# Normalised rows of a two-layer block made by ScalarE with a scale and a bias per row

## The reference

```python
def _layernorm(x, axis=-1, eps=1e-05):
    m = jnp.mean(x, axis=axis, keepdims=True)
    v = jnp.var(x, axis=axis, keepdims=True)
    return (x - m) / jnp.sqrt(v + eps)
...
    x = x + jnp.tanh(g_xattn[0]) * _L0_xattn_ref(16, 128, 256, L0_xattn_time_decay, L0_xattn_time_first, _layernorm(x, axis=-1), ctx_2048)
    x = x + jnp.tanh(g_ffn[0]) * _L0_ffn_ref(_layernorm(x, axis=-1), L0_ffn_W_q, ...)
    x = x + jnp.tanh(g_xattn[1]) * _L1_xattn_ref(_layernorm(x, axis=-1), ctx_2048, ...)
    x = x + jnp.tanh(g_ffn[1]) * _L1_ffn_ref(_layernorm(x, axis=-1), ...)
    return x
```

## Time and profile before

| | |
|---|---|
| median of 3 runs | 586.26 us (586.02 to 588.57) |
| the profiled execution | 589.14 us, of which the span 587.3 us |
| busy in the span | TensorE 477.8 us (81%), VectorE 402.3 us (68%), ScalarE 173.8 us (30%), GpSimd 144.1 us (25%) |
| TensorE's granted clock | 0.92 of full speed on average |

### The profile page before, as it was taken

One profiled execution on the slowest core, in us unless ns is written; L12 is line 12 of the kernel. 1 busy time (PEld: TensorE's weight loads), 2 busy tenths in 40 slices (PEclk: granted clock), 3 DMA queues, 4 the chain that ended last, 5 costly groups with the idle time before them and its releaser, 6 DMA issues.

```text
span 587.3 us, 7047 instructions
## 1 busy us (share of the span) xinstructions
PE 477.8 (81%) x2142; PEld 367.5 (63%) x2150; DVE 402.3 (68%) x1049; ACT 173.8 (30%) x363; POOL 144.1 (25%) x141
## 2 busy tenths in 40 slices
PE   1755989778999679899999979999868599999720
PEld 1432468656767567668776867777646487888510
DVE  6999777999868997867859683997825343223332
ACT  2601434121233111141222123213334147555210
POOL 4942113551104010000000010000275105004664
PEclk9857999989999889989999989999978699999775
DMA  8150012300000049000000000111121416555653
GB/s 296 69 186 0 2 30 93 94 1 0 2 0 1 1 135 304 1 1 0 2 1 0 2 0 28 54 55 54 64 90 71 127 36 195 165 168 171 180 182 123
DMA packets 34277, 43.79 MB, mean 75 GB/s; under 512 B 3009, under 2 KB 28098, under 8 KB 34242
## 3 DMA queue, kind: packets, MB, share of 16 engines
q1 hardware_dynamic: 31170, 34.96, 18.6%
q0 software_dynamic: 3072, 8.39, 4.7%
HBM read 24.99 MB, written 18.35 MB: 74 GB/s over the span
## 4 chain that ended last, share of the span: by engine, by line
PE 36%; issue 6%; POOL 5%; DVE 4%; DMA 3%; ACT 2%; POOLq 0%; SPq 0%; ACTq 0%; DVEq 0%
PE ring L600 6%; PE acc L564 5%; PE ring L751 3%; PE ring L820 2%; PE ring L767 2%; PE ring L619 2%; PE ring L540 2%; POOL x_rows L1456 2%; PE ring L541 2%; PE ring L542 2%; PE ring L800 2%; POOL q_f L1465 2%; PE ring L584 1%; DMA main_b<-x_rows 1%; PE ring L811 1%
## 5 line engine op out<-in xcount | busy, mean ns | idle before, releaser
L564 PE MATMUL acc<-w_down,act_s 128*128 128x256 f32 x384 | 91.0, 384 | 0.7 <-DVE act_s L1258 0.7
L564 PEld LDWEIGHTS acc<-w_down,act_s 128*128 128x128 f32 x384 | 73.9, 193 | 12.7 <-DVE act_s L1258 1.1
L540 PE MATMUL ring<-xt_h,up_l 128*128 128x512 f32 x160 | 72.3, 452 | 5.4 <-ACT logits L921 3.0
L1426 POOL TENSOR_TENSOR rstd<-var_eps,minus_half 128x4 f32<-128x4 f32 x16 | 16.6, 1035 | 215.5 <-DVE var_eps L1054 215.5
L541 PE MATMUL ring<-xt_l,up_h 128*128 128x512 f32 x160 | 65.0, 406 | 0.0
L542 PE MATMUL ring<-xt_h,up_h 128*128 128x512 f32 x160 | 64.9, 406 | 0.0
L971 ACT ACTIVATE act_s<-ring 128x512 f32<-128x512 f32 x48 | 28.7, 598 | 113.8 <-PE ring L542 113.8
L1241 DVE SCALAR_TENSOR_TENSOR act_s<-act_s,ring 128x512 f32<-128x512 f32 x48 | 32.7, 681 | 29.4 <-ACT act_s L971 22.6
L600 PE MATMUL ring<-up_e,act_s 128*128 x184 | 48.4, 409 | 4.7 <-issue 3.5
L1456 POOL DMA_INDIRECT x_rows<-main_a,slots x32 | 31.5, 985 | 64.5 <-ACT main_a L988 32.4
L600 PEld LDWEIGHTS ring<-up_e,act_s 128*128 128x128 f32 x184 | 35.7, 204 | 11.3 <-issue 6.9
(11 more groups left out here) (239 smaller groups left out, 948.6 us busy)
## 6 DMA issues: line engine op xcount, KB each, us to landing
main_b<-x_rows SPq DMA_DIRECT2D x22, 256.0 KB, 2.9
y_rows<-act_s SPq DMA_DIRECT2D x22, 256.0 KB, 2.2
x_rows<-k_r SPq DMA_DIRECT2D x1, 3968.0 KB, 14.5
x_nat<-in_x SPq DMA_DIRECT2D x8, 256.0 KB, 4.5
stage<-in_w_mlp SPq DMA_DIRECT2D x8, 256.0 KB, 2.7
up_e<-in_w_moe SPq DMA_DIRECT2D x8, 256.0 KB, 2.6
out_x<-x_nat SPq DMA_DIRECT2D x8, 256.0 KB, 2.3
x_rows<-k_r SPq DMA_DIRECT2D x1, 1920.0 KB, 19.7
```

Of the source, the lines that this page charges most:

```text
L540: pe.matmul(out, wl, xh, start=first, stop=False, skip_group_check=True)
L564: last = pe.matmul(acc[t // 2][:, t % 2, :], act_s[n % RING][:, tok], w_down[:, u, :], start=u == 0 and t % 2 == 0, stop=final, skip_group ...
```

## The change

ScalarE makes the rows of all norms but the very first (`wkv_in 0`) by 4 activations `Identity(scale * x + bias)` with scale = rstd and bias = -mean * rstd, where VectorE did. For the bias, VectorE writes `minus_mean` (one instruction more, while the two additions of eps become one), and GpSimd multiplies it by rstd after the power, having waited for its own power (`rstd_made`); only then is `rstd_ready` raised. rstd and the bias of `route_in` go straight to `rstd2` and `shift2`, so the copies of line 1069 are gone. In the list the steps keep their places.

```diff
+NORM_DVE = [("wkv_in", 0)]
...
+                if APPLY.get(kind) == part and step not in NORM_DVE:
+                    n = XN_ORDER[step]
+                    xn_free(act, n)
+                    act.wait_ge(rstd_ready, 1 + (LAST_STATS[g] if kind == "mlp_in" else STATS_ORDER[step]))
+                    seqs = main_seqs(g) if kind in ("mlp_in", "attn_in", "moe_in") else prep_seqs(g)
+                    for t, b in enumerate(seqs):
...
+                        last = act.activation(xn[n % 2][:, t, :], x_nat[:, b, :], ACT.Identity, bias=m, scale=r)
+                    last.then_inc(xn_ready, 1)
...
-                for p in range(2):
-                    b = seqs[2 * p]
-                    var = mean_rstd[:, b:b + 2, 1] if keep else mv[:, n, 2 * p:2 * p + 2, 1]
-                    last = dve.tensor_scalar(var_eps[:, n, 2 * p:2 * p + 2], var, LN_EPS, None, ALU.add)
-                last.then_inc(var_ready, 1)
...
+                dve.tensor_scalar(minus_mean[:, n, :].rearrange("p (q b) -> p q b", q=2), mean, -1.0, None, ALU.mult)
+                dve.tensor_scalar(var_eps[:, n, :].rearrange("p (q b) -> p q b", q=2), var, LN_EPS, None,
+                                  ALU.add).then_inc(var_ready, 1)
...
-                if step[0] == "route_in":
-                    for p in range(2):
-                        b = seqs[2 * p]
-                        last = dve.tensor_copy(rstd2[:, b:b + 2], rstd[:, o % 2, 2 * p:2 * p + 2])
-                    link(last)
...
-                elif APPLY.get(kind) == part:
+                elif APPLY.get(kind) == part and step in NORM_DVE:
                     normalize(step, seqs)
...
-                    pool.tensor_tensor(rstd[:, n % 2, :], var_eps[:, n % 2, :], minus_half[:, :],
-                                       ALU.pow).then_inc(rstd_ready, 1)
+                    r, m = scales(step)
...
+                    pool.tensor_tensor(r, halves[0], halves[1], ALU.pow).then_inc(rstd_made, 1)
+                    pool.wait_ge(rstd_made, n + 1)
+                    pool.tensor_tensor(m, halves[2], r, ALU.mult).then_inc(rstd_ready, 1)
```

More of the change, by code:

```diff
@@ L217 @@
 STATS_ORDER = {s[:2]: n for n, s in enumerate(s for s in SCHED if s[0] in APPLY and s[0] != "mlp_in" and s[2] == 0)}
+LAST_STATS = {f: max(n for s, n in STATS_ORDER.items() if s[0] == "route_in" and s[1] // 2 == MAIN_FIRST[f] % 8 // 4)
+              for f in range(NG)}
 ALL_UNITS = [("mlp", f, u) for f in range(NG) for u in range(MLP_UNITS)]
@@ L304, in build @@
         rstd = sb("rstd", [P, 2, GT])
+        shift = sb("shift", [P, 2, GT])
+        minus_mean = sb("minus_mean", [P, 2, GT])
         v_t = [sb(f"v_t{c}", [P, GN]) for c in range(C)]
@@ L469, in weigh_values, with by_prep, scales, xn_free @@
             return eng.tensor_tensor(va[:, 0], va[:, 1], v[c][:, :].rearrange("p (t j) -> p t j", t=GT), ALU.mult)
+        def by_prep(table, g):
+            if len(table.shape) == 3:
+                return table[:, :, :].rearrange("p (q b) t -> p q b t", q=2)[:, :, 2 * g:2 * g + 2, :]
+            return table[:, :].rearrange("p (q b) -> p q b", q=2)[:, :, 2 * g:2 * g + 2]
+        def scales(step):
+            if step[0] == "route_in":
+                return by_prep(rstd2, step[1]), by_prep(shift2, step[1])
+            n = STATS_ORDER[step] % 2
+            return tuple(table[:, n, :].rearrange("p (q b) -> p q b", q=2) for table in (rstd, shift))
+        def xn_free(eng, n):
+            if n >= 2:
+                prev = [s for s, k in XN_ORDER.items() if k == n - 2][0]
+                full(eng, (prev, "T", C - 1))
         def free_sem(key):
@@ L883, in _ @@
                 ee_a, ee_b = ee_a_of[g], ee_b_of[g]
-                if kind == "wkv_in" and part == 2:
+                if APPLY.get(kind) == part and step not in NORM_DVE:
[4 more added lines that the diff above has]
+                    for t, b in enumerate(seqs):
+                        if kind == "mlp_in":
+                            r, m = rstd2[:, b:b + 1], shift2[:, b:b + 1]
+                        else:
+                            r, m = (table[:, t // 2, t % 2:t % 2 + 1] for table in scales(step))
+                        last = act.activation(xn[n % 2][:, t, :], x_nat[:, b, :], ACT.Identity, bias=m, scale=r)
+                    last.then_inc(xn_ready, 1)
+                elif kind == "wkv_in" and part == 2:
                     if g == 0:
@@ L1425, in _ @@
                     pool.wait_ge(var_ready, n + 1)
[L1426 to L1427 removed]
+                    r, m = scales(step)
+                    halves = [table.rearrange("p (q b) -> p q b", q=2)
+                              for table in (var_eps[:, n % 2, :], minus_half[:, :], minus_mean[:, n % 2, :])]
+                    pool.tensor_tensor(r, halves[0], halves[1], ALU.pow).then_inc(rstd_made, 1)
+                    pool.wait_ge(rstd_made, n + 1)
+                    pool.tensor_tensor(m, halves[2], r, ALU.mult).then_inc(rstd_ready, 1)
                 elif kind == "wkv_in" and part == 2:
```

21 lines of the change are left out of this document (10 added, 11 removed).

## The result

The changed kernel takes 584.62 us (median of 20 runs, 582.69 to 588.59), the kernel before beside it 587.43 us (20 runs, 584.84 to 589.35). The ratio is 0.996, 95% interval 0.994 to 0.998: 0.4% or 2.4 us faster, within the 0.5% that counted as no change. A second comparison on another occasion gave 0.999, interval 0.998 to 1.001 (587.89 us, 12 runs, against 588.64). The forecast was 2.3 us faster, 584.0.

What follows compares the result with a forecast made beforehand. VectorE was taken as the bound at 14.5 to 57 and 110 to 142 us, elsewhere mostly TensorE or transfers. Places summed to -1.3 us, with clock terms -2.3, from 586.26 to 584.0 us; range 579.5 to 589.0.

Steps and rivals of the forecast that it cites:

- The likeliest case: Whole kernel: gains in the MLPs outweigh losses at the start and before the first MLP, -2.3 us; chance 0.52.
- Start: ScalarE's rows of wkv_in 1 delay the exponentials; VectorE's line 467 starts 2.1 us later, an idle 0.69 absorbed: +1.4 us.
- Before the first MLP: ScalarE's 8 rows delay the key/value evictions and TensorE, +1.4 us; the longer wait makes the clock fall, +1.1.
- First MLP: Rows of wkv_in 2 and mlp_in 1 leave VectorE's queue, so TensorE's waits of 4.00 and 1.50 us shrink: -2.8 us.
- the term of wkv_in 2: First MLP: its rows leave VectorE, 1.84 us less the overlap and ScalarE's slightly longer rows: 1.5 us gained.
- Second MLP: Multiplication and longer rows of route_in 2 cost +0.6 us; at its end 8 ScalarE rows delay a tanh, +0.4.
- Third MLP: Rows of attn_in 0 no longer hold up routing on VectorE, -1.3 us; full clock behind the shorter wait, -1.7.
- Fourth MLP: Rows of attn_in 2 come earlier, -1.3 us; 0.4 counted for the clock here and in the first MLP together.
- The end, +0.3: At attn_in 3 the multiplication stands in the queue of GpSimd's sends: +0.3 us.
- A dear bias: Rival: GpSimd's multiplication costs 1.04 us instead of 0.3, paid eight times, +3.6 us, 589.9; loss from 0.6 us on; chance 0.14.
- The rival that the relief of the first MLP is lost: TensorE's waits there hang on something else just behind: 2.8 us less gain, +0.5 us, 586.8; chance 0.14.
- the first rival, in which the relief goes further: Clock stays full behind all shortened waits and does not fall at 76 us: -6.4 us, 579.9; chance 0.20.

Runs made afterwards that it cites:

- all, with bias: Changed kernel with all rows made by VectorE again, as before the change, while GpSimd still makes every bias; ratio to the kernel before 1.000 (0.998 to 1.002).
- the values later: Changed kernel with wkv_in 2 and mlp_in 1 rows on VectorE, GpSimd weighing wkv_in 2's values only after VectorE reduced the routing's pair products; ratio to before 1.003.

## Why the prediction was right in sum and wrong in its parts

The likeliest case came true in sign, in size and in most of its places, and in the sum that was partly luck. The forecast of -2.3 us lies between the two profiles of the changed kernel, -5.6 and -1.9 us of span. The first MLP and the fourth gave 2.5 and 1.0 us more than their terms; the start lost 0.8 us more, and the low clock at 79 us up to 2.3 us more, by the execution.

- **Start**, predicted +1.4. Line 476 (467 before) started at 16.73 us, 2.2 later, as forecast. All of that ran through: the power of route_in 0 came at 57.15 instead of 54.95 us, 40.4 us behind that instruction in both kernels. With the bias alone ("all, with bias") it came at 55.68, and with wkv_in 1 back on VectorE at 55.89, so some 0.7 us is the bias and 1.3 the rows of wkv_in 1; route_in 0, which I had given nothing, cost nothing that shows (route_in 1 at 70.34 with both back, 70.37 with wkv_in 1 alone). The step that failed is the idle 0.69 us of VectorE at 20.80, which I took off. The gap is gone, but k_e behind it took 1.42 instead of 0.66 us. Both ended 0.28 us behind GpSimd's `q_f`, 21.46 behind 21.18 and 23.65 behind 23.37, and GpSimd had been moved by the same 2.2 us. So the gap was no slack, and it looks like the collision found in the first MLP; no experiment tests it here.
- **Before the first MLP**, predicted +1.4 for the wait and +1.1 for the clock. From the power to k_e it was 4.81 us and is 6.34, 1.5 more: right. The fall of the clock came as forecast. Its price was mis-sized: I priced one low stretch of 3.4 us, as the rows of before at 250 us had it. Seven profiles gave 25.2 to 28.6 us for the stretch, 27.0 in the mean, so against the 25.2 of the one with full clock 1.8 us on average for the clock and up to 3.4.
- **First MLP**, predicted -2.8. The step that failed is the term of wkv_in 2: 1.5 us predicted, 4.0 measured; that of mlp_in 1 was 1.3 and is 1.3. I counted the rows that go, and took the instructions behind them as they stood. The rows are right: they bring the two instructions of the routing 1.6 us nearer to the power. But those two and the comparisons behind them were slowed by GpSimd, and moving them forward took them out from under it: 1.9 us for the two, and 0.4 for the next (2.27 to 1.86). The kernel with the values later shows 2.0 us with the rows left on VectorE. The forecast wait of 2.5 us for the routing's transposes is gone altogether, and one of 2.18 us stands behind it. A clue was in the rows: the same rows of xn took 1.84 us beside GpSimd and 1.38 alone, and I used it for the rows only. The Trainium skill (GPSIMD Engine Reference, Key points) says that GpSimd and VectorE share their interfaces to the memory on the chip, and that instructions of VectorE with two inputs from it contend; the trace agrees, 0.42 against 1.46 us for a comparison of two inputs, while the reduction with one input took 0.42 us in both.
- **Second MLP**, predicted +0.6 and +0.4: 0.7 and 0.4. Right in size. Half of the 0.6 was to be the multiplication, and "all, with bias" shows none of it there (70.3 as before).
- **Third MLP**, predicted -1.3 for the rows and -1.7 for the clock: 1.3 and 1.6 where both came, 2.6 in the first profile. Right in the sizes. But the fall there does not hang on the wait alone as I had it: it came in two of three profiles with the long wait and in three of eleven with the short one.
- **Fourth MLP**, predicted -1.3 and a share of 0.4: -2.7. The wait was forecast at 2.3 us and is 2.36; the clock, at which I guessed 0.4 for this place and the first MLP together, gave 1.5. The end, +0.3, can't be seen: its stretch scatters from 193.8 to 197.1.
- **The rivals.** A dear bias is worse than I said: 1.04 us more cost 11 us where my count of eight places gives 8.3. The turning point that I put at 0.6 us lies near 0.5 by an estimate (0.28 and 2.4 us of gain by 11 us a us), and near 0.3 if the gain is the 0.4 us of the second comparison. The multiplication took 0.28 and is on the near side of it. The rival that the relief of the first MLP is lost fell, and of the first rival, in which the relief goes further, half came true: the clock stayed up behind the shortened waits, but it fell at 79 us.

Why 0.996 at one time and 0.999 at another can only be argued: the two profiles of the changed kernel part before 100 us, in the start (from 58.0 to 61.4 us the granted clock was 1.00 in the first and 0.52 in the second, and route_in 1 came 1.1 us later) and in the length of the low clock at 79 us, which stood there only in profiles with the wait of 3.5 us or more.

## What to carry to other kernels

Moving work from a full engine pays only at the places where that engine's queue is what the others wait for: five of nineteen norms carried all the gain that could be seen, and four others gave most of it back, above all those whose rows stood ahead of the evictions before the first MLP and ahead of the exponentials of the start, on an engine that had been free at the right moment. When a queue is shifted, look at what runs beside each of its instructions before and after, not only at what leaves it: a collision that ends was worth more here than the rows that were moved (2.4 against 1.6 us), and a gap of idle time in front of a collision was no slack. And an added 0.28 us on the way from moments to rows cost less than could be told, while 1.04 us more there cost tenfold.

## What the runs showed of the hardware

- A comparison and a multiplication of two tiles of 128 x 256 on VectorE took 0.42 us each alone, and 1.46 and 1.29 us beside GpSimd's multiplications of 128 x 512. The reduction of the same size took 0.42 us either way.
- Beside GpSimd, four of VectorE's instructions with two tiles as inputs (these two, and k_e at the start of before and of the changed kernel) all ended 0.28 us behind the end of the GpSimd instruction that ran when they began, whether that made them 0.66 or 1.46 us long.
- On 128 x 4 values, GpSimd's power takes 1.04 us and its multiplication 0.20 us: the operation, not the size, makes the power dear.
- The same wait of TensorE of 3.5 us went with a low clock of 0, 3.4, 6.8 or 10.2 us in different executions, worth 0 to 3.4 us. One profile of such a kernel can mislead by that much.
